# Two VectorE clips side by side, then the reciprocal, then the key rotation, in the first cross-attention of a two-layer decoder kernel

## The reference, cut to what matters

```python
q = (lat @ Wq).reshape(b, n, HEADS, DHEAD).transpose(0, 2, 1, 3)
k, v = jnp.split(ctx @ Wkv, 2, axis=-1)            # then reshaped to heads like q
k = apply_rope(k, cos[None, None], sin[None, None])
attn = jnp.einsum('bhnd,bhsd->bhns', q, k) * DHEAD ** (-0.5)
attn = jnp.clip(attn, -11.0, 11.0)
attn = jax.nn.softmax(attn, axis=-1)
out = jnp.einsum('bhns,bhsd->bhnd', attn, v)
out = out.transpose(0, 2, 1, 3).reshape(b, n, INNER)
return out @ Wo + bo
```

## Time and profile before

| what | us |
|---|---|
| median of 3 executions | 454.14 |
| lowest, highest | 453.61, 455.34 |
| profiled execution, its time | 454.88 |
| profiled execution, its span | 453.1 |
| TensorE busy in the span | 409.6 (90%) |
| VectorE busy | 289.1 (64%) |
| ScalarE busy | 205.2 (45%) |
| GpSimd busy | 194.7 (43%) |

### The profile page before, as it was taken

One profiled execution on the slowest core, in us unless ns is written; L12 is line 12 of the kernel. 1 busy time (PEld: TensorE's weight loads), 2 busy tenths in 40 slices (PEclk: granted clock), 3 DMA queues, 4 the chain that ended last, 5 costly groups with the idle time before them and its releaser, 6 DMA issues.

```text
span 453.1 us, 7698 instructions
## 1 busy us (share of the span) xinstructions
PE 409.6 (90%) x2882; PEld 275.1 (61%) x2882; DVE 289.1 (64%) x688; ACT 205.2 (45%) x290; POOL 194.7 (43%) x237
## 2 busy tenths in 40 slices
PE   4898999999999999989999977799779999999985
PEld 4676645455555456756899855444556555558974
DVE  4779976846766666643522978673688985246654
ACT  1676723243332333044323376657246455556550
POOL 3316647697777877332322447312452332100000
PEclk9989999999999999999999997999989999999999
DMA  8712000000004111160152005100000000010000
GB/s 299 310 35 83 1 0 2 1 1 0 1 0 187 48 46 48 56 232 0 71 87 41 2 18 74 22 3 3 0 2 3 2 3 2 2 33 5 0 1 23
DMA packets 8080, 19.78 MB, mean 44 GB/s; under 512 B 1958, under 2 KB 3974, under 8 KB 7526
## 3 DMA queue, kind: packets, MB, share of 16 engines
q1 hardware_dynamic: 8044, 19.30, 14.2%
HBM read 17.26 MB, written 1.15 MB: 41 GB/s over the span
## 4 chain that ended last, share of the span: by engine, by line
PE 70%; DVE 19%; issue 3%; POOL 3%; ACT 2%; DMA 2%; SPq 0%; DVEq 0%; POOLq 0%; ACTq 0%
PE ps L1678 67%; DVE big L1290 2%; DVE ps L1423 2%; DVE big L1299 2%; DVE mx_a L1427 2%; DVE big L1227 2%; DVE ps L1222 2%; DVE dtmp L1236 1%; DMA ident<-in_ident 1%; POOL big L743 1%; PE ps L1690 1%; PE ps L2075 1%; POOL rstd L638 1%; POOL big L657 1%; DMA late<-mid 1%
## 5 line engine op out<-in xcount | busy, mean ns | idle before, releaser
L1678 PE MATMUL ps<-big,late 128*32 128x256 f32 (+3 forms) x768 | 97.7, 382 | 7.7 <-DVE big L1299 4.9
L967 ACT ACTIVATE big<-ps 128x1024 f32<-128x1024 f32 x48 | 49.0, 1023 | 39.0 <-PE ps L1678 38.8
L1678 PE MATMUL ps<-late,big 128*128 128x128 f32 (+1 forms) x448 | 64.7, 275 | 2.0 <-DMA late<-mid 1.1
L1678 PEld LDWEIGHTS ps<-big,late 128*32 128x32 f32 (+2 forms) x768 | 35.9, 116 | 44.2 <-DVE big L1299 12.0
L1678 PEld LDWEIGHTS ps<-late,big 128*128 128x128 f32 (+1 forms) x448 | 46.9, 151 | 20.0 <-issue 11.5
L703 POOL TENSOR_TENSOR big<-big 128x512 f32<-128x512 f32 x31 | 43.0, 1397 | 19.5 <-DVE big L1299 19.4
L1290 DVE RECIPROCAL big<-ps 128x256 f32<-128x256 f32 x16 | 28.1, 1757 | 33.3 <-PE ps L1678 33.3
L907 ACT ACTIVATE big<-ps 128x1024 f32<-128x1024 f32 x32 | 31.0, 1022 | 39.9 <-PE ps L1678 39.9
L636 POOL TENSOR_SCALAR vareps<-meanvar 128x2 f32<-128x2 f32 (+2 forms) x13 | 2.9, 226 | 106.3 <-DVE meanvar L1121 102.6
L1423 DVE CUSTOM_DVE_ANT_0 ps<-ps,big 128x512 f32<-128x512 f32 x64 | 42.9, 705 | 7.8 <-PE ps L1678 6.6
L929 ACT ACTIVATE big<-ps 128x512 f32<-128x512 f32 x32 | 19.1, 597 | 36.7 <-PE ps L1678 36.7
(11 more groups left out here) (261 smaller groups left out, 748.3 us busy)
## 6 DMA issues: line engine op xcount, KB each, us to landing
attn_w<-in_w_x SPq DMA_DIRECT2D x1, 2560.0 KB, 13.3
big<-parts_kx SPq DMA_DIRECT2D x18, 128.0 KB
late<-in_w_up SPq DMA_DIRECT2D x1, 2048.0 KB, 7.6
late<-in_w_dn SPq DMA_DIRECT2D x4, 512.0 KB, 4.0
attn_w<-in_w_up SPq DMA_DIRECT2D x1, 1024.0 KB, 5.0
attn_w<-in_w_dn SPq DMA_DIRECT2D x1, 1024.0 KB, 7.0
big<-mid SPq DMA_DIRECT2D x24, 32.0 KB, 1.8
parts_kx<-ctx_r SPq DMA_DIRECT2D x1, 768.0 KB, 3.2
```

The costliest lines, as they stand in the source:

```text
L967: nc.scalar.activation(ex1[:, n % 3, :].rearrange("p (r n) -> p r n", r=2), ps[:, 2 * (n % 2):2 * (n % 2) + 2, :], ACT.Exp, scale=scale).t ...
L1678: return nc.tensor.matmul(o, lhsT, rhs, start=start, stop=stop, skip_group_check=shared)
```

## The change

On VectorE both clips of an entry stand together, then comes the `normed0` of that entry for the head pair before; the key rotation is the last thing in a head pair. The `normed0(c, 0)` that stood at the end of its own head pair now stands after the first two clips of the next one. On GpSimd the add that ends the rotation stands behind the second total. No instruction is added or removed, and TensorE's, ScalarE's and SyncE's lists are as before.

```diff
@@ -709,7 +709,7 @@
                         pool.wait_ge(S["o0_ps"], 2 * (c - 1) + b + 1)
                     nc.gpsimd.tensor_tensor(etot[:, b, :], esum[:, 0, :], esum[:, 1, :], ALU.add
                                             ).then_inc(S["e0_tot"], 1)
-                if u == 2 and K_FIRST + c < B * NPAIR:
+                if u == 3 and K_FIRST + c < B * NPAIR:
                     rotated0(K_FIRST + c)
             root("post1")
             pool.wait_ge(S["r0_max"], 1)
@@ -1292,19 +1292,17 @@
                                         ).then_inc(S["o0_norm"], 1)
 
             for c in range(NPAIR):
-                for u in range(4):
-                    n = 4 * c + u
-
-                    dve.wait_ge(S["e0_exp"], n + 1)
-                    nc.vector.tensor_scalar(ex(n), ex(n), float(np.exp(CLIP)),
-                                            float(np.exp(-CLIP)), ALU.min, ALU.max
-                                            ).then_inc(S["e0_clip"], 1)
-                    if u == 2 and K_FIRST + c < B * NPAIR:
-                        rotary(K_FIRST + c)
-                    if u == 3:
-                        normed0(c, 0)
-                    if u == 1 and c:
-                        normed0(c - 1, 1)
+                for b in range(B):
+                    for n in range(4 * c + 2 * b, 4 * c + 2 * b + 2):
+                        dve.wait_ge(S["e0_exp"], n + 1)
+                        nc.vector.tensor_scalar(ex(n), ex(n), float(np.exp(CLIP)),
+                                                float(np.exp(-CLIP)), ALU.min, ALU.max
+                                                ).then_inc(S["e0_clip"], 1)
+                    if c:
+                        normed0(c - 1, b)
+                if K_FIRST + c < B * NPAIR:
+                    rotary(K_FIRST + c)
+            normed0(NPAIR - 1, 0)
             normed0(NPAIR - 1, 1)
             add_and_norm(6, "y0_ps", 1, 3, "post1")
 
```

## The result

The changed kernel took 450.0 us in the median of 8 runs (447.31 to 452.21); the kernel before, in 8 runs of the same comparison, 455.21 us (453.61 to 460.88). The ratio is 0.988, with a 95% interval from 0.9844 to 0.9916: faster by 0.8 to 1.6%. The prediction said 447.7 us and 446.8 to 450.7, and a gain of 6.4 us, 1.4%.

The account below looks back on a forecast made before the run. TensorE was taken to bound the attention, standing for late VectorE clips. Six waits of 1.04 us plus 0.17 in the tail gave 6.4 us, so the median goes from 454.14 to 447.7 us, range 446.8 to 450.7.

Parts of the forecast that it names:

- Six waits of 1.04 us: Head pairs 1 to 6: TensorE's second mix no longer stands for a late VectorE clip, saving 6 x 1.04 us.
- The tail, 0.17 us: Step 15, mix of unit 30: GpSimd's sum is ready earlier with the clip ahead of `normed0(6, 1)`, saving 0.17 us.
- The rotation last costs nothing: VectorE, end of head pair: rotation ends at 160.5, TensorE wants the banks at 162.37; 1.9 us in hand, no cost.
- the slack of the second reciprocal: Before the odd step's first mix: about 0.7 us in hand, 0.2 left if one GpSimd sum holds off the second clip.
- GpSimd's add last costs nothing: Rotation's add behind the second total: the close case, key tile 15 read in step 14, has 1.8 us in hand; no cost.
- The sum, 6.4 us: Total gain in the attention: 6 x 1.04 + 0.17 = 6.4 us, with all that follows moving as one piece.
- One unknown: VectorE-GpSimd port: a GpSimd sum between the clips may delay the second; price 0 to another 1.27 us, taken as 0.
- rival A: GpSimd adds delay the second clip 1.0 to 1.7 us; mixes wait up to 0.5 us, six times: 450.7 us; chance 0.13.
- A's sign: In the profile after: TensorE waits for line 1291 before odd steps' first mix; second-place clips take 1.3 us or so.
- rival C: A whole GpSimd add precedes each clip; first mix stands 0.4 us more, 6 x 0.4 = 2.2 us slower, 456.3; chance 0.04.
- The 0.9 us either way: Whole-kernel time: scatter allowance from three runs' spread, 453.61 to 455.34; it set the range's lower end, 446.8.

Follow-up runs that it names:

- one moved call: Kernel before with only the rotation moved one place later, behind the clip of unit 4c+3: stretch 102.09 us, median 450.99 us, ratio 0.9892.
- The run without a gap: Changed kernel, but the first clip of an entry waits for both units' exponentials: stretch 101.82 us, median 449.36 us, ratio 0.9855.

## Why the prediction was right, point by point

**Six waits of 1.04 us: right.** All six are gone, head pairs 2 to 5 run at 11.44 to 11.45 us where 11.46 was forecast, and in 6 TensorE doesn't stand either. That the clip's lateness was due to what stood ahead of it on VectorE is shown from two sides: one moved call removes it (stretch 102.09), and GpSimd's part alone does nothing (108.24).

**The tail, 0.17 us: right.** The seam of unit 30 is 0.92 us in the profile after (180.74 - 179.82) and was 1.06, so 0.14 us went.

**The rotation last costs nothing: right**, and so is the step that made it part of the argument, the slack of the second reciprocal. The forecast was 0.2 us with one add between the clips; 0.12 was measured by moving the rotation (0.27 by the rows of the profile after), and the rotation ahead of that reciprocal costs 6.9 us of stretch (108.72 - 101.83).

**GpSimd's add last costs nothing: right.** No stand in step 14 with the clips early; 0.42 us once with the clips late.

**The sum, 6.4 us: 0.5 us too large for the stretch** (5.93 measured). The step that failed is the one headed "One unknown": I took 0 for the port, since in the middle of the attention the delay fits the slack. It does there, but the working was made for one head pair in the middle and never for the first ones, where GpSimd came from an add of 2.25 us with its sums and totals close behind. There a sum and a total both held the clips, and the prediction had this case as rival A, for all six head pairs. It came in one. Its price, 0.5 us a time, was right. That it came once and not six times was not worked out: the long second clips that the prediction gave as A's sign came in the middle of the attention too (1.67 us), and there the slack covered them with 0.12 us to spare. The forecast was right there by a narrow margin.

**A reading that was wrong without harm.** Against rival C I said that VectorE keeps the port over two clips in a row when the second is ready. The run without a gap shows the opposite: two ready clips of 2.37 us with an add between them; so does the changed kernel at 157.04 (2.36 us for two). In the earlier trace rows VectorE kept it; which of the two comes is not settled by these runs. One row had been made into a rule. Rival C's own sum is rounded unevenly as well: by its terms it is 6 x 0.35 = 2.1 us, where 6 x 0.4 stands beside 2.2.

**The time.** The profiled run moved by 454.88 - 447.8 = 7.1 us, the medians by 5.2 (or, by the ratio, 5.5). The forecast of 447.7 us stands within the runs of the changed kernel (447.31, 447.8 are its lowest two) and 2.3 us below its median. Of these 2.3 us, 0.5 are head pair 1, and 1.1 are the starting point: I had taken the median of three runs of the kernel before, 454.14, as its time, and with more runs it was 455.2 to 455.5. The other 0.7 are within the scatter of the rest, which the forecast took for fixed and which goes with TensorE's clock: the profiled run had a mean granted clock of 0.986, the two runs around the median of 450.0 us had 0.979. The 0.9 us either way, read from three runs, was too small for it, as the changed kernel's eight runs span 4.9 us. That the median lies in the range at all is owed to the range reaching up to rival A's 450.7; by the time alone the forecast could not be told from A. What shows the mechanism right is the stretch, and the 5.9 us between runs at the same clock.

## What to carry to other kernels

When the bound engine waits for a short instruction whose input was ready long ago, look at what stands ahead of it in its own engine's list, above all at a wait for something later: here moving one call of 1.2 us gave nearly all of the gain. Then ask what has the least slack in the new order and work it out for the first rounds of a loop too, not only for one in the middle, since the other engines may enter the loop late. A gain of half a microsecond can be judged by the length of its own stretch in the profile when the whole time scatters by several, and the whole times by comparing runs with the same mean granted clock.

## What the runs showed of the hardware

- VectorE's clip and GpSimd's add exclude each other for a whole instruction (clips of 0.68 us alone and 1.67 us beside an add, the median back at 694 ns with the adds made small). The Trainium skill ("SBUF — State Buffer", section "Who interferes with whom") says so too: the one that issues first keeps the port and the other blocks. What I had not expected: an add that waits can get in between two clips that are both ready (2.37 us for two), and did not in another place (1.28 us for two with an add of 2.25 us held beside them). Which of the two happens stays open.
- The granted clock of TensorE fell from 2.4 to 1.2 GHz in two to four places behind the attention while TensorE still had work, in different places from one profile to the next of the same instructions. The rest was 259.2 to 259.6 us with 7 us at the lower clock, 260.1 to 260.3 with 10, 261.3 to 262.4 with 14, and 263.1 to 263.9 with 17.
